# A mixture-of-experts and time-mix block: expert biases added by gathers, eight row buffers, weights queued behind x

## What is computed

```python
xn = layernorm(x)
# time mix: k, v, r are products of xn with 256x256 weights
#   wkv is a scan over the tokens with time_decay and time_first
attn = (sigmoid(r) * wkv) @ out_w.T
# experts: two of eight per token, weights from a softmax of xn @ gate_w.T + gate_b
out_e = (silu(xn @ w1[e].T + b1[e]) * (xn @ w3[e].T + b3[e])) @ w2[e].T + b2[e]
y = sum(weight[t, e] * out_e for the two experts of t)
z = silu(xn @ ws1.T + bs1) * (xn @ ws3.T + bs3) @ ws2.T + bs2     # shared expert
return x + attn + y + z
```

## Time and profile before

| | |
|---|---|
| three runs | 469.54, 473.65, 474.9 us; median 473.65 |
| the profiled execution | 470.54 us, span 468.8 us |
| mean granted clock of TensorE | 0.981 |
| busy: PE, DVE, ACT, POOL | 95%, 78%, 51%, 50% |
| stages in the trace | `route` to about 60 us, `run_experts` to 259, `mix` to the end |

### The profile page before, as it was taken

How to read it: one execution, slowest core, us unless ns; L and a number is a source line. 1 busy time by engine, 2 the same in 40 slices (tenths; PEclk the granted TensorE clock), 3 DMA queues, 4 the chain that set the end, 5 groups by cost and what they waited for, 6 DMA issues and landing times.

```text
span 468.8 us, 8342 instructions
## 1 busy us (share of the span) xinstructions
PE 445.1 (95%) x2549; PEld 374.1 (80%) x2549; DVE 365.1 (78%) x680; ACT 239.8 (51%) x394; POOL 232.5 (50%) x224
## 2 busy tenths in 40 slices
PE   5898977979999999999998999999999999999997
PEld 4453746858888888888887879798888889898987
DVE  5968868798776987878675689996968687877863
ACT  4778735677768586876754532423324142324031
POOL 3234777354858658589744477661523425160000
PEclk9899769999999999999999999999999999999999
DMA  8999743255674854344454863726152433431001
GB/s 245 396 351 285 211 115 94 66 199 203 237 264 120 273 183 139 125 136 135 119 198 158 290 238 113 251 68 228 50 185 86 155 122 123 157 119 63 25 24 45
DMA packets 45874, 77.24 MB, mean 165 GB/s; under 512 B 5924, under 2 KB 32268, under 8 KB 45836
## 3 DMA queue, kind: packets, MB, share of 16 engines
q1 hardware_dynamic: 36924, 55.83, 33.8%
q0 software_dynamic: 8240, 20.88, 16.9%
q10 hardware_dynamic: 672, 0.04, 0.1%
HBM read 48.52 MB, written 28.21 MB: 164 GB/s over the span
## 4 chain that ended last, share of the span: by engine, by line
PE 46%; POOL 18%; issue 13%; DVE 10%; DMA 4%; ACT 4%; SPq 3%; POOLq 0%; DVEq 0%; ACTq 0%
POOL xg L1005 8%; PE ps_w L1540 5%; PE ps_w L1542 5%; PE ps_w L1541 5%; PE ps_w L1605 5%; PE ps_w L1606 5%; PE ps_w L1607 5%; PE ps_g L1082 4%; DMA w_lo<-w_all 3%; POOL den L1017 2%; PE ps_y L1082 2%; SPq L424 2%; POOL den L1016 2%; DVE stats L687 2%; POOL firsts L1024 2%
## 5 line engine op out<-in xcount | busy, mean ns | idle before, releaser
L1005 POOL DMA_INDIRECT xg<-xn_rows,tile_tok x71 | 71.4, 1006 | 21.9 <-issue 19.1
L1516 POOL DMA_INDIRECT yg<-expert_rows,rows x64 | 66.8, 1044 | 23.6 <-issue 17.1
L1082 PE MATMUL ps_g<-w_hi,x_hi 128*128 x142 | 56.7, 399 | 1.6 <-DVE x_lo L1237 1.6
L1082 PE MATMUL ps_g<-w_lo,x_hi 128*128 x142 | 56.7, 399 | 0.0
L1082 PE MATMUL ps_g<-w_hi,x_lo 128*128 x142 | 56.3, 397 | 0.0
L1647 ACT ACTIVATE sact<-ps_w,vec_b 128x512 f32<-128x512 f32 x32 | 22.0, 687 | 58.7 <-PE ps_w L1542 58.7
L1540 PE MATMUL ps_w<-col_hi,s_hi 128*128 128x512 f32 x128 | 50.5, 395 | 0.4 <-DVE shid L1758 0.4
L1542 PE MATMUL ps_w<-col_hi,s_lo 128*128 128x512 f32 x128 | 50.2, 392 | 0.0
L1541 PE MATMUL ps_w<-col_lo,s_hi 128*128 128x512 f32 x128 | 50.1, 392 | 0.0
L1082 PE MATMUL ps_y<-w_hi,h_hi 128*128 x142 | 43.1, 304 | 1.3 <-DVE h_lo L1253 1.3
L1246 DVE TENSOR_TENSOR hid<-ps_g,act 128x512 f32<-128x512 f32 (+1 forms) x36 | 23.7, 657 | 25.5 <-ACT act L1158 25.5
(11 more groups left out here) (247 smaller groups left out, 1278.5 us busy)
## 6 DMA issues: line engine op xcount, KB each, us to landing
expert_rows<-y SPq DMA_DIRECT2D x35, 256.0 KB, 2.2
w_lo<-w_all SPq DMA_DIRECT2D x16, 384.0 KB, 10.1
table<-mix_tables SPq DMA_DIRECT2D x8, 768.0 KB, 6.7
xT<-x SPq DMA_DIRECT2D x16, 256.0 KB, 6.1
xn_rows<-xn SPq DMA_DIRECT2D x16, 256.0 KB, 9.2
xn_columns<-xT SPq DMA_DIRECT2D x8, 512.0 KB
col<-xn_columns SPq DMA_DIRECT2D x8, 512.0 KB, 5.0
res<-x SPq DMA_DIRECT2D x16, 256.0 KB, 2.9
```

The costliest lines, as they stand in the source:

```text
L1005: pool.indirect_dma_start(out=xg[b][:, t, :], out_offset=None, in_=xn_d[:, :], in_offset=bass.IndirectOffsetOnAxis(ap=tile_tok[:, first_ti ...
L1082: mm = nc.tensor.matmul(out, x[:, k, :], w[:, ds(e, 1), k, cols].rearrange("p o n -> p (o n)"), start=(k == 0 and n == 0), stop=(last and ...
L1516: pool.indirect_dma_start(out=yg[a.buf(2)][:, k, q, :], out_offset=None, in_=y_d[:, :], in_offset=bass.IndirectOffsetOnAxis(ap=picked[a.bu ...
```

## The change

Three things are changed together.

- The biases b2 are no longer a product on PE. `b_all` is now nine rows in DRAM: the shared bias, then the experts' in falling order. `route` keeps the place (`rank`) that marks each chosen expert and puts it as a row number (`bias_row`) beside `slots` into one tile, `picks`. In `mix`, POOL's `prepare` gathers the expert rows as before, waits until they have landed, gathers the bias rows with an add onto the same bytes (`add_biases`, L1438 of the new kernel), and adds the shared bias to `res` (`add_shared`, L1446). DVE's `experts` waits for these two. `terms`, `gT`, `g_now`, `rows`, `rows_hi`, `rows_b`, their splits, transposes and matmuls are gone.
- `xn` has eight buffers (NN = NSTEP), and the waits for a free buffer are gone.
- SP's queue: all 16 weights stand right behind x, the 16 stores behind them. DVE makes six low parts (LOW = 6) instead of two ahead of the expert stage.

```diff
-        NN = 4
-        MADE, BOTH, HIGH, LOW = 4, 6, 13, 2
+        NN = NSTEP
+        MADE, BOTH, HIGH, LOW = 4, 6, 13, 6
...
-            arriving = iter(ARRIVAL)
-            for _ in range(AHEAD):
-                load_w(next(arriving))
+            for i in ARRIVAL:
+                load_w(i)
...
-                at_least(dve, s_T, a.i - NN + 1)
-                at_least(dve, s_xout[a.buf(NN)], a.uses(NN) * 32)
...
+            nc.vector.tensor_copy(tile_exp[:], exp_f[:]).then_inc(s_ready, 1)
+            own.link(nc.vector.reciprocal(gates[:, 0, :], red[:]))
             dve.wait_ge(s_gate, 1)
             nc.vector.tensor_tensor(gates[:, 1, :], gates[:, 1, :], gates[:, 0, :], ALU.mult)
...
+            nc.vector.tensor_scalar(bias_row, rank[:], 1.0, float(E), ALU.max, ALU.min).then_inc(s_ready, 1)
...
-            def pick(a):
-                at_least(pool, b_o, a.i * Q - Q)
-                nc.gpsimd.tensor_copy(g_now[a.buf(2)][:], gT[:, ds(a.i, 1), :].rearrange("p o n -> p (o n)")
-                                      ).then_inc(b_gc, 1)
+            def add_biases(a):
+                pool.wait_ge(b_gath[a.buf(2)], (a.uses(2) + 1) * 16 * TOPK * Q)
+                pool.sem_inc(b_go, 1)
+                for k in range(TOPK):
+                    for q in range(Q):
+                        pool.indirect_dma_start(
+                            out=yg[a.buf(2)][:, k, q, :], out_offset=None, in_=b_all,
+                            in_offset=bass.IndirectOffsetOnAxis(ap=picked[a.buf(2)][:, TOPK + k, q:q + 1], axis=0),
+                            compute_op=ALU.add
+                        ).then_inc(b_rows[a.buf(2)], 16)
+
+            def add_shared(a):
+                pool.wait_ge(b_res[a.buf(2)], (a.uses(2) + 1) * 32)
+                nc.gpsimd.tensor_tensor(res[a.buf(2)][:], res[a.buf(2)][:],
+                                        shared_b[:, None, :].broadcast_to([P, Q, C]), ALU.add).then_inc(b_bias, 1)
+
+            def prepare(a):
+                gather(a)
+                add_biases(a)
+                add_shared(a)
 
             def step(a, first, left):
-                pick(a)
                 if left > 0:
-                    gather(a.plus(1))
+                    prepare(a.plus(1))
...
                 def mixed(q):
-                    nc.tensor.matmul(ps_w[q][:, 0:C], g_now[a.buf(2)][:], rows_b[:, q, :],
-                                     start=True, stop=False)
...
                 if g == 0:
-                    dve.wait_ge(b_res[buf], (a.uses(2) + 1) * 32)
-                    dve.wait_ge(b_gath[buf], (a.uses(2) + 1) * 16 * TOPK * Q)
+                    dve.wait_ge(b_bias, a.i + 1)
+                    dve.wait_ge(b_rows[buf], (a.uses(2) + 1) * 16 * TOPK * Q)
```

More of the change, by code:

```diff
@@ L55 @@
 EPS = 1e-5
-TERMS = 32
 PIECE = 256
@@ L164, in build @@
             route_sync, route_gpsimd, route_tensor, route_scalar, route_vector, placed = route(
[L165 to L166 removed]
+                nc, kept, x, first, decay, vec_tf, vec_td, gate_w, gate_b, w_all, w_first, nw_d, xn_d, xT_d, ident, slots, bias_row, gates,
+                  tile_tok, tile_exp, w_hi, w_lo, lane_i, row_of1, minus)
             raw_s13 = sb("raw_s13", [P, KC, 2 * SF], F32)
@@ L224, in _, with route @@
                 mix_vector(dve)
-def route(nc, kept, x, first, decay, vec_tf, vec_td, gate_w, gate_b, w_all, w_first, nw_d, xn_d, xT_d, ident, slots, gates,
-          tile_tok, tile_exp, w_hi, w_lo, terms, lane_i, row_of1, minus):
+def route(nc, kept, x, first, decay, vec_tf, vec_td, gate_w, gate_b, w_all, w_first, nw_d, xn_d, xT_d, ident, slots, bias_row, gates,
+          tile_tok, tile_exp, w_hi, w_lo, lane_i, row_of1, minus):
     with ExitStack() as ctx:
@@ L568, in scalar @@
                 split(i)
[L569 to L572, removed]
             for i in range(4, BOTH):
@@ L984, in sync @@
                     sp.dma_start(*loads[a - A_LOADS]).then_inc(c_ld, 16)
-                if a == A_ROWS:
-                    sp.wait_ge(c_zero, 1)
-                    for q in range(Q):
-                        sp.dma_start(rows[TERMS * q:TERMS * q + 3 * E + 2, q, :], b_all).then_inc(c_rows, 16)
                 if a == 4 * LAST_V + 1:
@@ L1118, in tensor @@
             pe.wait_ge(s_both, BOTH)
-            pe.wait_ge(s_terms, 5)
-            for i in range(NSTEP):
-                mm = nc.tensor.transpose(ps_y[i // 4][:].rearrange("p t c -> p (t c)")[:, i % 4 * P:(i % 4 + 1) * P],
-                                         terms[:, i * Q:(i + 1) * Q, :].rearrange("p q n -> p (q n)"), ident[:])
-                if i % 4 == 3:
-                    mm.then_inc(c_turn, 1)
+            pe.wait_ge(s_ready, 1)
             es[0] = experts(0)
@@ L1194, in scalar @@
             cut_x(0)
-            for h in range(2):
-                act.wait_ge(c_turn, h + 1)
-                nc.scalar.activation(gT[:, 4 * h:4 * h + 4, :].rearrange("p j n -> p (j n)"),
-                                     ps_y[h][:].rearrange("p t c -> p (t c)"), ACT.Copy).then_inc(c_gT, 1)
             silu(0)
@@ L1217, in scalar @@
                     halves(v)
-                if a == A_HI:
-                    act.wait_ge(c_rows, 16 * Q)
-                    act.wait_ge(c_zero, 1)
-                    nc.scalar.activation(rows_hi[:], rows[:], ACT.Copy).then_inc(c_rhi, 1)
                 if a == DUOS - 4:
@@ L1365, in vector, with mix @@
                     differences(v + 1)
-                if a == A_ZERO + 2:
-                    low_mask()
-        return sync, gpsimd, tensor, scalar, vector, (c_y, c_yc, c_wlo, c_gT, c_rowsb)
-def mix(nc, kept, over, x, xT_d, y_d, y_stored, coef_stored, tab_d, out, slots, gates, vr_hi, vr_lo, raw_s13, raw_o, raw_s2,
-        col0, col_hi0, col_lo0, vec_b1, vec_b3, gT, rows_b):
+        return sync, gpsimd, tensor, scalar, vector, (c_y, c_yc, c_wlo, (c_ld, len(loads)), s_ready)
+def mix(nc, kept, over, x, xT_d, y_d, y_stored, coef_stored, tab_d, out, picks, b_all, shared_b, gates, vr_hi, vr_lo, raw_s13, raw_o,
+        raw_s2, xT, x_hi, x_lo, vec_b1, vec_b3):
     with ExitStack() as ctx:
@@ L1424, in mix @@
         b_xlo = sem("b_xlo")
-        b_gc = sem("b_gc")
+        b_rows = [sem(f"b_rows{b}") for b in range(2)]
+        b_bias = sem("b_bias")
         b_v = sem("b_v")
@@ L1510, in gather @@
                 at_least(pool, b_slot, a.i * TOPK - TOPK)
-                nc.gpsimd.tensor_copy(picked[a.buf(2)][:], slots[:, :, ds(a.i * Q, Q)]).then_inc(b_idx, 1)
+                nc.gpsimd.tensor_copy(picked[a.buf(2)][:], picks[:, :, ds(a.i * Q, Q)]).then_inc(b_idx, 1)
                 pool.wait_ge(b_idx, a.i + 1)
```

118 lines of the change are left out of this document (28 added, 90 removed).

## The result

The changed kernel takes 543.39 us (median of four runs, 540.30 to 547.06) against 471.6 us of the kernel before, run beside it (469.13 to 474.9): a ratio of 1.152, interval 1.141 to 1.163. The profiled execution took 542.63 us. So the forecast's direction and mechanism held, and its sum came out 13 us short: near the top of its range, above the 540 us that its dearest price for an add gives, and inside only by the margin that was left above that price.

What follows compares the result with a forecast made beforehand. PE bounds the last stage now; POOL would bound it after the change, at 31.0 us a step. First set, seven further steps, an 18 us tail and 1.74 us beyond the span give 529.5 us; range 491 to 545, its own 520 to 545.

Steps and rivals of the forecast that it cites:

- PE's saving: Last stage: bias matmuls (L1573) leave PE, 0.12 us each, 3.8 us in all or 0.48 us a step.
- Rival 3: Adds of L1438 so cheap that POOL keeps up and PE bounds: not slower, down to 464 us; chance 3%.
- Rival 1: Adds cost little more than plain gathers, L383's 1.545 us coming from 2 KB rows: 491 to 510 us; 20%.
- p: POOL's price of one bias add, issue plus 0.30 us gap: taken as 1.85 us, range 1.25 to 2.01.
- The landing wait: POOL, each step of the last stage: waits until the last gather has landed before the adds, 1.85 us.
- The shared sum: POOL, each step of the last stage: adding the shared bias over 128x1024, 2.4 us.
- The tail: What follows DVE's request for the eighth set, to the span's end: 18 us, about 2 of them low clock.
- The head: Everything ahead of the last stage: a gain of 1.3 + 0.5 + 0.9 = 2.7 us.
- rival 4: First stage: stores land after 59.3 us, so first gathers wait; 5 us late gives 535 us; chance 4%.
- part (b): First stage: weights right behind x; first gathers about 1.3 us earlier, PE's first product about 0.5 us more.
- Part (c): Expert stage: PE's waits for h_lo not counted as unrelated to the biases, 0.9 us won.
- Rival 2: Last stage: PE's clock stays low through each waiting step, PE bounds at 50 us a step, 658 us; 3%.

Runs made afterwards that it cites:

- the old head: Changed kernel without bias adds and shared sum, with the first stage of the kernel before (four buffers, old load order): 467.44 us.
- split wait: Changed kernel, whole computation, gathers of the two halves k on two semaphores, so adds start after the first four gathers land: 527.01 us.
- no sum: Changed kernel without POOL's sum of the shared bias onto res (L1446), the bias adds kept: 523.17 us.
- plain gathers: Changed kernel with the 64 gathers of bias rows writing the rows instead of adding them: 503.42 us.
- with pairs: Changed kernel, whole computation, table of expert-pair bias rows, four 2 KB adds a step instead of eight, landing wait split: 490.26 us.

## Why the prediction was right, and where its sum was short

- **PE's saving.** Forecast 0.48 us a step; without biases a step is 0.34 to 0.38 us shorter (25.40 to 25.06, 25.68 to 25.30), 2.9 us over eight steps instead of 3.8. Nearly right, and hidden behind POOL in the changed kernel.
- **The rule that fell.** The Trainium skill, "DMA: Bandwidth & Descriptors", section "Anatomy of one DMA — SWDGE (gpsimd) path", calls descriptor generation small; the trace disagrees here too, with 1.54 us of POOL for each add. Rival 3 rested on that and is out.
- **Rival 1** put the price of the 2 KB adds down to their rows. It is out: 1 KB costs 1.541 us at the median. The choice of L383's row for p was right in kind.
- **The adds** came out right in the sum, and partly by luck. I took the median, 1.545; the mean is 1.68 (107.4 us in all), 8.6 us more. Against that, the gap of 0.30 us stands seven times in a set and not eight, since the landing wait takes the place of the first (2.4 us), and the sum begins half a microsecond before the row of the last add ends (4.4 us). From the first add's start to the sum's start the eight sets take 120.0 us, where 64p is 118.4.
- **Why some adds are long.** Of the 64, 11 take 1.98 to 2.58 us, 8 us above the rest together. Each of them began while DVE was at a product or sum whose inputs all lie in SBUF, as the add at 311.50 did beside this row:

```profile
310.82 1.22 DVE L1670 TENSOR_TENSOR col_lo<-col,col_hi 128x1024 fp32r<-128x1024 f32 x1
```

  Each ended 1.40 to 1.45 us after that DVE row did; here 313.48 after 312.04. Rows of DVE that read a product of PE (the tiles `ps_v` and `ps_w`) had no such effect. The long gathers agree (0.81 to 0.89 us after the DVE row), in the other runs too. No run takes these DVE rows away, so the cause is argued from this agreement.
- **The landing wait is the term that was too small.** It was taken as 1.85 us from a median landing; it took 23.5 us over eight sets, 2.9 each: 8.7 us short, the largest part of the miss. In five sets the last gather did land 2.7 to 2.8 us after its issue began, as forecast, but POOL's next row starts about 0.8 us after the landing, in every set. The chain of waits in the third set:

```profile
337.43 2.78 DMA yg<-expert_rows,rows
...
340.25 0.83 issue
341.09 1.57 POOL yg L1438
```

  In the other three sets, the first two and the last, the landing itself took 3.5 to 4.1 us.
- **The shared sum** was taken as 2.4 us and takes 2.3 of a step (323.96 to 326.25, the next copy), though its row lasts 2.9. That was right.
- **The ends.** POOL's first copy stood at 260.05 (259.8 in the forecast), and DVE began the eighth set at 521.42 (509.8). Of these 11.6 us the landing waits make about 8.7, the adds 1.6, the copies and gathers 0.9 and the late start 0.25. The tail took 19.5 us, not 18: after its wait PE was granted 0.50 of its clock to 525 us and 0.60 from there to 530, and twelve products stand 0.43 us apart there, against 0.23 at the full clock. 11.6 + 1.5 = 13.1 us, the whole miss.
- **The head** is a term that came out by accident. The profile of the changed kernel has 2.4 us of it, but only 1.0 by my reasons. Timelines of DVE, POOL and PE there:

```profile
60.03 0.20 DVE L810 TENSOR_SCALAR tile_tok<-tok_f 128x71 int32<-128x71 f32 x1
...
61.35 1.00 POOL L962 DMA_INDIRECT xg<-xn_rows,tile_tok  x1 [16.64 <-DMA xn_rows<-xn]
...
66.46 0.49 PE L1024 MATMUL ps_g<-w_hi,x_hi 128*128 x1 [1.25 <-DVE x_lo L1164]
```

  POOL was free, as forecast, but the list was ready a microsecond later than before, the stores landed at 60.45 and not near 55 (rival 4, in part), and the first gather stood at 61.35, where I had 59.6. The eight transposes gave nothing: the first product follows the first rows after 1.67 us (from 64.79) and did so after 1.66 before, since it waits for DVE's `x_lo`. So of part (b) only 0.3 us is left, the earlier first product (66.46 against 66.76). Another 1.0 us came from the granted clock: the first six products run at the high level here, where before they ran at the low one. The stretch of the changed kernel that answers to the earlier trace rows:

```profile
66.00:68.00 2.00, 1.54 (x7) 1.23 (x8) 1.08 (x2) 0.00 (x0) 1.59 (x2) 1.00 0.31 90
```

  Part (c), 0.9 us, did come out: before, PE waits 0.64 us for `h_lo` at 231.87, and the expert stage gains 1.0 us at that place in each of six profiles without the bias products, the one with the old head among them. In nine other profiled executions with the new head `values` of step 0 starts between 257.81 and 260.37 us, around the 259.19 of before (256.76 in this one). With the old head against the new the difference was 0.05 us. So of the 2.7 us the 1.8 of part (b) are to be read as nothing. This is also why 464 us was not reached without both biases: 471.3 - 1.0 - 2.9 = 467.4.
- **Rival 2** (a low clock sets the pace) is out: the waiting steps from the third on have 0.87 to 0.97 of the clock, and POOL steps of 30.5, 29.6 and 27.3 us instead of 32.16 (split wait, no sum, plain gathers) went with times of 527, 523 and 503 us, until PE bound at full clock.

## What to carry to other kernels

When work moves from the engine that bounds to one with slack, lay out the whole list of the receiving engine for one step, its waits for landing among it, each counted up to the start of the engine's next row, and sum means, not medians. Do the same once more for the first steps, where the slack of the steady state has not yet been built up: with pairs POOL had 3 us of slack a step and still lost 21 us in two sets. And price the whole of the gain first by leaving the work out: here it was 0.9%.

## What was not expected of the hardware

- An indirect add costs POOL 1.54 us, an indirect gather 0.95, nearly whatever the rows: 64 instead of 128 rows 1.41 us, 512 values instead of 256 1.57 (medians). Fewer, longer rows are the way to make them cheap for POOL, though the longer ones land later: 5.6 us after the issue instead of 4.3.
- A POOL sum over SBUF stopped a DVE subtraction outright (3.36 us instead of 1.23, until the sum was over). The other way round, an add or a gather that POOL began beside such a DVE row lasted up to 1 us longer. The Trainium skill, "SBUF — State Buffer", section "SBUF: two separate sides", describes this: the two engines share a pair of ports that one of them holds for a whole instruction while the other blocks. The trace agrees, and shows the price where PE had no lead: 3.5 us for one such meeting, 1.4 of it by the low clock that PE was granted after its wait.
- The same first stage is followed by an expert stage at either level of the granted clock, 1.2 or 2.4 GHz in its first products: the second product follows the first after 0.32 us in the changed kernel's profile and after 0.59 us in that without the adds. Of ten profiled executions with this first stage it was the only one that began at the high level.
